# Two head groups in one output bank, one spread product for the softmax denominators, and a two-product projection in a four-layer attention kernel

## The reference

```python
# layer 0: cross attention, both sides normalized and modulated
q  = (ada_ln(x) @ Wq + bq);  kv = (ada_ln(ctx) @ Wkv + bkv)
out = softmax(q k^T / sqrt(8)) v          # per head, over 1601 keys
x  = x + (out @ Wp + bp)
# layers 1 and 2: gated self attention, cross attention, gated MLP
x = x + g_sa * (attend(qkv of modulated ln(x)) @ sa_proj_w + sa_proj_b)
x = x + (attend(ln(x), context) @ ca_proj_w + ca_proj_b)   # layer 2 norms the context
x = x + g_ff * (gelu(mod(ln(x)) @ fc1 + b) @ fc2 + b)
```

## Time and profile before

| | us |
|---|---|
| median of 3 runs | 6937.63 (6933.79 to 6939.47) |
| the profiled execution | 6946.5 |
| its span in the trace | 6944.7 |
| PE busy | 6345.0 |
| DVE busy | 4541.3 |
| ACT busy | 4288.9 |
| POOL busy | 975.2 |

### The profile page before, as it was taken

How to read it: one execution, slowest core, us unless ns; L and a number is a source line. 1 busy time by engine, 2 the same in 40 slices (tenths; PEclk the granted TensorE clock), 3 DMA queues, 4 the chain that set the end, 5 groups by cost and what they waited for, 6 DMA issues and landing times.

```text
span 6944.7 us, 161117 instructions
## 1 busy us (share of the span) xinstructions
PE 6345.0 (91%) x51334; PEld 3295.9 (47%) x51334; DVE 4541.3 (65%) x10086; ACT 4288.9 (62%) x8318; POOL 975.2 (14%) x1660
## 2 busy tenths in 40 slices
PE   6999999999888899999999788799999999979998
PEld 3444444444555444444444355444444444434554
DVE  5777777777555677777777255477777777724333
ACT  3676676676655577777776355477777777632223
POOL 3112121121111111110110011121122112100000
PEclk9999999999999999999999899899999999989998
DMA  2221222222111222222221011222222222100110
GB/s 86 73 65 54 73 64 55 72 61 54 43 52 55 73 75 66 69 57 72 75 68 40 12 52 54 65 61 61 77 65 58 70 76 64 47 31 29 52 41 24
DMA packets 181125, 406.34 MB, mean 59 GB/s; under 512 B 16992, under 2 KB 124560, under 8 KB 166416
## 3 DMA queue, kind: packets, MB, share of 16 engines
q1 hardware_dynamic: 180752, 400.67, 21.3%
HBM read 317.47 MB, written 83.14 MB: 58 GB/s over the span
## 4 chain that ended last, share of the span: by engine, by line
PE 74%; DVE 10%; issue 6%; ACT 6%; DMA 1%; POOL 1%; DVEq 0%; ACTq 0%; SPq 0%; POOLq 0%
PE bank L1114 17%; PE bank L1087 16%; PE bank L1070 15%; DVE MX L1413 3%; PE bank L1037 2%; PE bank L1044 2%; PE bank L652 2%; PE bank L1050 2%; PE bank L1032 2%; ACT P L1244 2%; PE bank L1102 2%; PE bank L643 2%; PE bank L669 1%; PE bank L1055 1%; PE bank L581 1%
## 5 line engine op out<-in xcount | busy, mean ns | idle before, releaser
L1244 ACT ACTIVATE P<-bank 128x512 f32<-128x512 f32 (+1 forms) x5504 | 3084.9, 597 | 1495.7 <-PE bank L1070 1465.9
L1413 DVE TENSOR_REDUCE MX<-bank 128x1 f32<-128x400 f32 (+1 forms) x6144 | 3214.2, 569 | 1133.5 <-PE bank L1087 1056.1
L1070 PE MATMUL bank<-QP,KP 128*128 128x256 bf16 (+1 forms) x11008 | 2089.7, 276 | 107.1 <-ACT QP L1256 44.6
L1087 PE MATMUL bank<-KP,QP 96*128 96x400 bf16 (+1 forms) x6144 | 2097.5, 342 | 88.7 <-DMA QP<-scr_q 42.6
L1114 PE MATMUL bank<-P,VA 128*9 128x256 f32 (+1 forms) x22016 | 1724.8, 385 | 54.9 <-ACT RS L1251 42.1
L1070 PEld LDWEIGHTS bank<-QP,KP 128*128 128x128 bf16 (+1 forms) x11008 | 1033.9, 101 | 778.9 <-issue 180.7
L1087 PEld LDWEIGHTS bank<-KP,QP 96*128 96x128 bf16 x6144 | 593.7, 97 | 1058.2 <-DVE MX L1413 642.8
L1114 PEld LDWEIGHTS bank<-P,VA 128*9 128x9 f32 (+1 forms) x22016 | 327.8, 88 | 769.3 <-issue 661.9
L1416 DVE TENSOR_REDUCE MX<-bank 128x2 f32<-128x512 f32 x512 | 326.8, 686 | 297.1 <-PE bank L1091 290.2
L1536 POOL COPY VA<-VN 128x416 f32<-128x416 f32 (+1 forms) x320 | 132.4, 414 | 2593.7 <-PE bank L1114 1330.2
L1256 ACT CAST QP<-bank 2x512 bf16<-2x512 f32 x640 | 338.8, 575 | 87.2 <-PE bank L1102 81.9
(11 more groups left out here) (208 smaller groups left out, 5294.7 us busy)
## 6 DMA issues: line engine op xcount, KB each, us to landing
KP<-scr_k SPq DMA_DIRECT2D x192, 900.6 KB
QP<-scr_q SPq DMA_DIRECT2D x960, 48.0 KB
CN<-ctx_n SPq DMA_DIRECT2D x40, 768.0 KB
scr_k<-KSF SPq DMA_DIRECT2D x48, 600.8 KB, 3.3
scr_k<-KSF SPq DMA_DIRECT2D x48, 600.0 KB, 3.3
CT<-ctx_t SPq DMA_DIRECT2D x24, 800.5 KB, 4.4
KP<-scr_ks SPq DMA_DIRECT2D x128, 144.0 KB
scr_q<-QS SPq DMA_DIRECT2D x80, 192.0 KB, 2.1
```

The lines of the kernel that those rows point to most:

```text
L1070: last = nc.tensor.matmul(SC[ph.score_bank(2 * (g * ph.nt + t) + half)][0:kt, k * N:(k + 1) * N], KP[g][:, c0:c0 + kt], QP[g][:, h * N:(h ...
L1087: last = nc.tensor.matmul(dst[:, 0:n], QP[g][0:MR, h * N + qt * 128:h * N + qt * 128 + 128], KP[g][0:MR, h * ph.nk + c0:h * ph.nk + c0 + n ...
L1244: nc.scalar.activation(P[v % 2][0:kt, half * 2 * N:(half + 1) * 2 * N], SC[ph.score_bank(2 * (g * ph.nt + t) + half)][0:kt, :], ACT.Exp, s ...
L1413: nc.vector.tensor_reduce(MX[:, r, c:c + 1], src[:, 0:CHUNKS[c][1]], AX.X, ALU.max).then_inc(sem("max_done"), 1)
```

## The change

Two groups (a pair, NPAIR = 2) now share the output bank and its partitions. The weights VA of a probability product have 18 columns for each head: an even group has its 9 in the first half and zeros in the second, an odd group the other way round. The bank is started by the first tile of an even group and stopped by the last of an odd one, and then holds values and sums of both at partitions 32h to 32h+17. ACT copies it once for a pair. RS and ON are one tile of 128x512 each. Piece d is one product of the 0-1 matrix `spread` (128x128) with all of RS: each partition gets the sum that belongs to it. DVE takes the reciprocal of the whole bank, 128x512, and multiplies RS by it. e0 and e1 are gone; y is two products and stands in slot 9 (self: 3). Two counters (`inverse_ready`, `group_done`) become one (`heads_scaled`), for which ACT's copy of the first pair of the next element waits. The biases of the projections, folded once at the start, take 10 products in place of 20. In the changed file the products of d and y are on lines 1039 and 1043, the reciprocal and the multiplication on 1371 and 1373.

```diff
@@ class Phase, Element @@
-            heads_copied=NG, group_done=NG, inverse_ready=1, max_full=self.nm * NG, max_done=self.nm * NG,
+            heads_copied=NPAIR, heads_scaled=1, max_full=self.nm * NG, max_done=self.nm * NG,
...
-                at = dict(d=3, e0=5, e1=9, y=11) if ph.cross else dict(d=1, e0=3, e1=4, y=4)
+                at = dict(d=3, y=9) if ph.cross else dict(d=1, y=3)
...
-        VA = [sb("VA%d" % k, [128, len(CROSS_TILES), G, HD + 1], f32) for k in range(2)]
+        VA = [sb("VA%d" % k, [128, len(CROSS_TILES), G, 2 * (HD + 1)], f32) for k in range(2)]
...
-        RS = [sb("RS%d" % g, [128, N], f32) for g in range(NG)]
-        ON = [sb("ON%d" % g, [128, N], f32) for g in range(NG)]
-        REC = sb("REC", [128, N], f32)
-        RDN = sb("RDN", [128, 2 * H], f32)
-        RDX = sb("RDX", [128, 2 * NG * 128], f32)
+        RS = sb("RS", [128, NPAIR * N], f32)
+        ON = sb("ON", [128, NPAIR * N], f32)
@@ TensorE: piece @@
                 elif name == "d":
-                    pe.wait_ge(sem("heads_copied"), at("heads_copied", b, NG))
-                    for g in range(NG):
-                        for qt in range(2):
-                            c = (2 * g + qt) * G
-                            last = nc.tensor.matmul(MISC[:, c:c + G], RS[g][:, qt * 128:(qt + 1) * 128], w("pick"),
-                                                    start=True, stop=True)
-                elif name[0] == "e":
-                    pe.wait_ge(sem("inverse_ready"), at("inverse_ready", b, 1))
-                    for k in range(4):
-                        c = (4 * int(name[1]) + k) * 128
-                        last = nc.tensor.matmul(MISC[:, k * 128:(k + 1) * 128], RDX[:, c:c + 128], w("ident"),
-                                                start=True, stop=True)
+                    pe.wait_ge(sem("heads_copied"), at("heads_copied", b, NPAIR))
+                    last = nc.tensor.matmul(MISC[:, :], w("spread"), RS[:, :], start=True, stop=True)
                 elif name == "y":
-                    pe.wait_ge(sem("group_done"), at("group_done", b, NG))
-                    for g in range(NG):
-                        last = nc.tensor.matmul(MISC[:, 0:N], w(ph.name + "wp", g * D, D), ON[g][:, :],
-                                                start=(g == 0), stop=(g == NG - 1))
+                    pe.wait_ge(sem("heads_scaled"), at("heads_scaled", b, 1))
+                    for p in range(NPAIR):
+                        last = nc.tensor.matmul(MISC[:, 0:N], w(ph.name + "wp", p * D, D), ON[:, p * N:(p + 1) * N],
+                                                start=(p == 0), stop=(p == NPAIR - 1))
@@ TensorE: head_values @@
-                    pe.wait_ge(sem("heads_copied"), at("heads_copied", b, g))
+                    if g % 2 == 0:
+                        pe.wait_ge(sem("heads_copied"), at("heads_copied", b, g // 2))
...
-                    last = nc.tensor.matmul(OB[32 * h:32 * h + HD + 1, 0:N], VA[g % 2][0:kt, t, h, :],
+                    last = nc.tensor.matmul(OB[32 * h:32 * h + 2 * (HD + 1), 0:N], VA[g % 2][0:kt, t, h, :],
                                             P[(g * ph.nt + t) % 2][0:kt, h * N:(h + 1) * N],
-                                            start=(t == 0), stop=(t == ph.nt - 1))
+                                            start=(g % 2 == 0 and t == 0), stop=(g % 2 == 1 and t == ph.nt - 1))
@@ ScalarE: copy_heads and its calls @@
-            def copy_heads(ph, b, g):
-                at = ph.c.at
-                act.wait_ge(sem("pv_done"), at("pv_done", b, (g + 1) * ph.nt))
-                wait(act, "group_done", at("group_done", b, g + 1 - NG))
-                nc.scalar.copy(RS[g][:, :], OB[:, 0:N]).then_inc(sem("heads_copied"), 1)
+            def copy_heads(ph, b, p):
+                act.wait_ge(sem("pv_done"), ph.c.at("pv_done", b, (2 * p + 2) * ph.nt))
+                nc.scalar.copy(RS[:, p * N:(p + 1) * N], OB[:, 0:N]).then_inc(sem("heads_copied"), 1)
...
-                        if t == 0 and g:
-                            copy_heads(ph, b, g - 1)
-                        elif t == 0 and el.prev:
-                            copy_heads(*el.prev, NG - 1)
+                        if t == 0 and g == 2:
+                            if el.prev:
+                                act.wait_ge(sem("heads_scaled"), el.prev[0].c.at("heads_scaled", el.prev[1], 1))
+                            copy_heads(ph, b, 0)
+                        elif t == 0 and g == 0 and el.prev:
+                            copy_heads(*el.prev, 1)
@@ VectorE: piece @@
                 elif name == "d":
                     dve.wait_ge(sem("misc_full"), use + 1)
-                    nc.vector.reciprocal(RDN[:, :], MISC[:, 0:2 * H]).then_inc(sem("misc_free"), 1)
+                    nc.vector.reciprocal(ON[:, :], MISC[:, :]).then_inc(sem("misc_free"), 1)
                     dve.wait_ge(sem("misc_free"), use + 1)
-                    nc.vector.tensor_scalar(RDX[:, :].rearrange("p (h r) -> p h r", r=32),
-                                            RDN[:, :].unsqueeze(2).to_broadcast([128, 2 * H, 32]), 1.0, None,
-                                            ALU.mult).then_inc(sem("inverse_ready"), 1)
-                elif name[0] == "e":
-                    dve.wait_ge(sem("misc_full"), use + 1)
-                    for k in range(2):
-                        g = 2 * int(name[1]) + k
-                        last = nc.vector.tensor_tensor(ON[g][:, :], RS[g][:, :], MISC[:, k * N:(k + 1) * N], ALU.mult)
-                    last.then_inc(sem("misc_free"), 1)
-                    dve.wait_ge(sem("misc_free"), use + 1)
-                    dve.sem_inc(sem("group_done"), 2)
+                    nc.vector.tensor_tensor(ON[:, :], RS[:, :], ON[:, :], ALU.mult).then_inc(sem("heads_scaled"), 1)
@@ weights made on the host: strips, main @@
-        p = np.zeros((4, 32, NG, m.shape[1]), f)
-        p[:, :HD] = m.reshape(NG, 4, HD, -1).transpose(1, 2, 0, 3)
+        p = np.zeros((4, 32, NPAIR, m.shape[1]), f)
+        for s in range(2):
+            p[:, (HD + 1) * s:(HD + 1) * s + HD] = m.reshape(NPAIR, 2, 4, HD, -1)[:, s].transpose(1, 2, 0, 3)
...
-            "pick": (k[:, None] == 32 * np.arange(G)[None, :] + HD).astype(f),
+            "spread": (k[:, None] == k[None, :] // 32 * 32 + np.where(k[None, :] % 32 // (HD + 1) == 1, 2 * HD + 1, HD))
+            .astype(f),
```

More of the change, by code:

```diff
@@ L23 @@
 NG = H // G
+NPAIR = NG // 2
 R9 = 9 * HD
@@ L56, in _columns @@
     cols, at = {}, 0
-    main = [("mean", D), ("pick", G), ("ident", D), ("eps5", 1), ("eps6", 1), ("one", 1)]
+    main = [("mean", D), ("spread", D), ("ident", D), ("eps5", 1), ("eps6", 1), ("one", 1)]
     for a in ATT:
-        main += [(a + "wq", D), (a + "wk", D), (a + "wv", D), (a + "wp", NG * D), (a + "bv", NG),
+        main += [(a + "wq", D), (a + "wk", D), (a + "wv", D), (a + "wp", NPAIR * D), (a + "bv", NPAIR),
                  (a + "bq", 1), (a + "bk", 1), (a + "bp", 1)]
@@ L184, in __init__ @@
             if prev:
-                pieces += [(0, "post", n) for n in ("d", "e0", "e1", "y")]
+                pieces += [(0, "post", n) for n in ("d", "y")]
         else:
             if prev:
-                at = dict(d=3, e0=5, e1=9, y=11) if ph.cross else dict(d=1, e0=3, e1=4, y=4)
+                at = dict(d=3, y=9) if ph.cross else dict(d=1, y=3)
                 pieces += [(at[n], "post", n) for n in at]
@@ L1158, in _ @@
                         for k, a in enumerate(ATT):
-                            for g in range(NG):
-                                last = nc.tensor.matmul(bank[0][:, k:k + 1], w(a + "wp", g * D, D),
-                                                        w(a + "bv", g, 1), start=(g == 0), stop=(g == NG - 1))
+                            for p in range(NPAIR):
+                                last = nc.tensor.matmul(bank[0][:, k:k + 1], w(a + "wp", p * D, D),
+                                                        w(a + "bv", p, 1), start=(p == 0), stop=(p == NPAIR - 1))
                         last.then_inc(sem("bias_full"), 1)
@@ L1293, in _ @@
                     if ph.el["after"]:
-                        copy_heads(ph, B - 1, NG - 1)
+                        copy_heads(ph, B - 1, 1)
                 elif isinstance(ph, MlpPhase):
@@ L1305, in _ @@
             for k in range(2):
-                nc.vector.memset(VA[k][:, :, :, :], 1.0)
+                nc.vector.memset(VA[k][:, :, :, (HD + 1) * k:(HD + 1) * (k + 1)], 1.0)
+                nc.vector.memset(VA[k][:, :, :, (HD + 1) * (1 - k):(HD + 1) * (2 - k)], 0.0)
             nc.vector.memset(VN[:, FULL, :], 0.0)
@@ L1536, in pack_values @@
                 nc.gpsimd.tensor_copy(
-                    VA[g % 2][:, 0:ph.nt, :, 0:HD],
+                    VA[g % 2][:, 0:ph.nt, :, (HD + 1) * (g % 2):(HD + 1) * (g % 2) + HD],
                     VN[:, 0:ph.nt, G * HD * g:G * HD * (g + 1)].rearrange("p t (h d) -> p t h d", d=HD)).then_inc(
```

## The result

The changed kernel takes 6951.68 us (median of 16 runs, 6945.08 to 6959.64) where the kernel before, run beside it, takes 6938.43 (16 runs, 6930.17 to 6951.48). The ratio is 1.0018, with a 95% interval of 1.001 to 1.0026: no gain, and a small loss. The forecast was 6861 us, its range 6780 to 6965.

What follows compares the result with a forecast made beforehand. PE bounds c1, DVE a0 and c2 in slots 5 to 11, the query-to-load chain self attention. Terms -27 + 0 - 25 - 30 + 15 - 4 - 6 = -77 us; less 8.9 from profiled to median, 6861 us, range 6780 to 6965.

Steps and rivals of the forecast that it cites:

- c1, -27: Cross-attention loop c1, where PE sets the pace: each round 1.8 us shorter over 15 rounds, 27 us gained.
- First PE is 0.9 early, then it stands 2.85 longer: c1's first head group: shorter d puts PE 0.9 us ahead, then DVE's longer block holds it 2.85, net +1.95.
- a0 and c2, 0: Cross-attention loops a0 and c2, where DVE sets the pace in slots 5 to 11: net 0 over 31 rounds.
- From there DVE runs without a gap: a0 and c2 after slot 6's maxima: DVE stays busy, PE savings gain nothing; shift rows about 0.3 us later.
- Self attention, -25: Self-attention loops s1 and s2: 0.8 us gained in each of 31 rounds, 25 us in all.
- 0.7 us late; of that 0.1 to 0.7 reaches the query: Self round: variance product waits for d's bank until the reciprocal ends, 0.7 us late, delaying the query 0.1 to 0.7.
- 1.5 us of slack: Self round: keys arrive at 4175.7, the first maximum starts at 4177.27; that gap is all that can be won.
- a0's back edge, -30: PE's instruction-fetch stall at the start of a0's rounds: 30 us gained, taken between bounds of nothing and 78.
- The rival that it is cured: a0's instruction-fetch stall at its back edge vanishes: 78 us gained instead of 30, 6813 us; chance 0.22.
- The fourth: Self-attention and weight gains fail: 18-column loads +29, self +25, perhaps a0 and c2 +15; about 6925 us; chance 0.16.
- The third: Instruction-fetch stall moves to c2 as well and a0 gives nothing back: slower, 6969 us; chance 0.14.
- rival of a short reciprocal: DVE's reciprocal takes 0.7 us, no block: c1 gains 38, a0 and c2 59, self attention 22; 6742 us; chance 0.08.

## Why the prediction was wrong

The rounds of the table above against the terms of the sum:

- **The reciprocal's length**, 3.2 us by the slope of two rows: right (3.35).
- **c1, -27.** The round grew by 1.1 us instead of falling by 1.8. The failed step is "First PE is 0.9 early, then it stands 2.85 longer": the stop came (3.31 us, had 0.31), and the step ended there. Behind it PE ran at half its clock for 7 us, worth some 2.1 us by the run with the stop filled. That is most of the 2.9 us by which the step was off, 46 us over 16 rounds; of the rest 0.4 is the 18 columns, by the run without them, and 0.4 stays open. The text named "a lower clock at times" for self attention alone, though a0 had both already: stops of 2.8 us and a clock of 0.97.
- **a0 and c2, 0.** c2 lost 1.7 us a round, though its fetches had gone. The failed step is "From there DVE runs without a gap": with PE at half clock behind its stop, DVE has read its queue of maxima and then waits for PE's next ones. In this c2 round, which began at 5108.0:

```profile
5122.07 0.69 DVE L1373 TENSOR_TENSOR ON<-RS,ON 128x512 f32<-128x512 f32 x1
5126.06 0.57 DVE L1394 TENSOR_REDUCE MX<-bank 128x1 f32<-128x400 f32 x1 [0.86 <-PE bank L1075]
5128.43 0.57 DVE L1394 TENSOR_REDUCE MX<-bank 128x1 f32<-128x400 f32 x1 [0.27 <-PE bank L1075]
5129.69 0.58 DVE L1394 TENSOR_REDUCE MX<-bank 128x1 f32<-128x401 f32 x1 [0.69 <-PE bank L1075]
...
5140.34 0.61 PE L1090 MATMUL bank<-IDB,NMB 128*2 128x128 bf16 x8 [1.52 <-DVE NMB L1409]
```

  DVE stood 1.8 us in three gaps, and the shift rows came 32.3 us into the round. Before, they came 30.3 into it (5242.53), so they were 2.0 late where the step had 0.3. In a0 the run with the stop filled measured this part: clock 1.00, and 1.4 us less a round. For c2 itself it isn't measured, since that run had fetches there.
- **Self attention, -25.** It cost 0.5 to 0.7 us a round. The failed step is "0.7 us late; of that 0.1 to 0.7 reaches the query". The variance product stood 2.30 us, and the first maximum then waited for a load issued late:

```profile
4144.80 0.69 PE L1014 MATMUL bank<-SQ,W 128*128 128x256 f32 x2 [2.30 <-DVE ON L1371]
...
4157.62 0.82 SPq L957 DMA_DIRECT2D KP<-scr_ks  x1
...
4162.37 0.61 PE L1079 MATMUL bank<-KP,QP 96*128 96x256 bf16 x4 [1.77 <-DMA QP<-scr_q]
```

  From issue to maximum it is 4.75 us, as the earlier trace rows had it. Counted from the mean product of the round (means of 12 rounds of s2), the variance product starts at 6.95 us where it was 5.96, the load is issued at 19.8 for 18.4, and the first maximum starts at 24.5 for 24.7. So 1.4 us of the "1.5 us of slack" went to the delay, and 0.2 was won. The loss lies behind the maximum: 6.2 us to the next mean product for 5.4 before. After that wait PE's granted clock is 0.73, where it was 1.00 in the same stretch before (4177.20 on):

```profile
4162.30:4168.60 6.30, 5.60 (x45) 2.75 (x46) 3.02 (x8) 2.91 (x6) 0.24 (x1) 0.73 0.33 102
4177.20:4182.70 5.50, 4.55 (x47) 2.49 (x46) 3.08 (x8) 4.08 (x9) 0.24 (x1) 1.00 0.32 102
```

  That the clock makes this loss wasn't tested by a run in self attention. The slack of "1.5 us, all that can be won" was also too small: with d behind the query the round fell to 4.4 us below the kernel before. What the wait for the load hid was that the whole chain from variance to store could start earlier.
- **a0's back edge, -30.** The rival that it is cured came true as well: before, a0's round was 5.1 us longer than c2's, now they are equal (102.38 and 102.35), so 71 us over 14 rounds against 78 forecast for that case. It did not exclude the failures above: the cases were treated as exclusive, and the good one and the bad ones came together.
- **The weights, +15**: right (16).
- **The rivals.** The fourth (6925) came nearest: it had self attention gain nothing and a0 and c2 lose 0.5 us a round, but no loss in c1. The third did not come: no "issue" wait shows among PE's in c2. Two slips change nothing: the five chances add up to 1.02, and 6915 + 15 is 6930.

Summed, 46 (c1) + 31 x 1.7 (a0 and c2) + 31 x 1.4 (self) less 41 (the back edge, 71 for 30) is 101 us above the forecast; measured were 91. The rival of a short reciprocal was given 6742, 119 under the forecast. The multiply-add in its place, fetches cured besides, came to 6645, 307 under the changed kernel. That price of the long reciprocal is what the forecast underrated: it is more than the DVE time itself, 80 blocks of 2.67 us or 214.

## What to carry to other kernels

Price a long operation by what is queued behind it, and then by the engine that it stops: a stop of 3 us of TensorE in each round cost the stop and some 7 us at half clock after it. A redundant layout (here 16 copies of each reciprocal) is cheap for a matrix product and dear for an operation that is paid by the column; try the engine with a table for it. What stands ahead of the next element's load decides a short loop's time, so finish the old element behind the new one's query.

## What the runs showed of the hardware

- A reciprocal of 512 columns takes 3352 ns on VectorE, one of 32 columns 351: 6.25 ns a column. Ln and Exp of the same shape take 594 and 630 ns on ScalarE.
- A loop of 1930 instruction records of TensorE (counted in the trace between two branches) fetched no instructions in its rounds, or nine blocks in each, by 128 records of code ahead of it. The price was 3.0 us a round there, and 0.8 to 2.5 in the loops of 1958 and 1960 records. The same loop with 20 records more fetched after a shift of 20, and not after one of -40.
- After a stop of 3.31 us in a c1 round TensorE's granted clock was 0.50 for some 7 us; with 3 us of products that nobody reads put into the stop it stayed at 1.00, and the round was 2.1 us shorter.
